# A vision-tower kernel on one core: low-rank coefficients and lora_b as scaled fp16 halves, transposed by DMA

## The reference, cut to what matters

```python
def reference(x, log_dt, B, inv_A_real, A_imag, attn_W, attn_b, W, b, A, Bm, Wr):
    h = s4d_kernel(log_dt, C=x, B, inv_A_real, A_imag, L=1024)     # (32, 128, 1024)
    h = h + layernorm(h) @ attn_W.T + attn_b
    z = layernorm(h)
    gates = softmax(z @ Wr.T)                                      # 4 experts
    proj = einsum('bsi,eri->bser', z, A)                           # 4 experts x rank 8
    lora_out = einsum('bser,eor->bseo', proj, Bm)
    mix = einsum('bse,bseo->bso', gates * 2.0, lora_out)
    return h + (z @ W.T + b) + mix
```

## Time and profile before

| what | value |
|---|---|
| median of 3 runs | 821.04 us |
| the profiled execution's own time | 821.13 us |
| its span in the profile | 819.3 us |
| TensorE busy (PE) | 777.7 us, 95% |
| VectorE busy (DVE) | 625.9 us, 76% |
| ScalarE busy (ACT) | 527.2 us, 64% |
| GpSimd busy (POOL) | 6.5 us, 1% |
| DMA packets of the SP queue | 40.0% of 16 engines |

### The profile page before, as it was taken

One profiled execution on the slowest core, in us unless ns is written; L12 is line 12 of the kernel. 1 busy time (PEld: TensorE's weight loads), 2 busy tenths in 40 slices (PEclk: granted clock), 3 DMA queues, 4 the chain that ended last, 5 costly groups with the idle time before them and its releaser, 6 DMA issues.

```text
span 819.3 us, 14989 instructions
## 1 busy us (share of the span) xinstructions
PE 777.7 (95%) x5390; PEld 389.9 (48%) x5390; DVE 625.9 (76%) x1250; ACT 527.2 (64%) x884; POOL 6.5 (1%) x21
## 2 busy tenths in 40 slices
PE   2758789999999999999999999999999999999998
PEld 2634344444444444444444444444444444444443
DVE  6679797877788778777787778777887787778532
ACT  5667786757676676767766675767757676765210
POOL 2000000000000000000000000000000000000000
PEclk9979999999999999999999999999999999999999
DMA  7837652545233333433324333433324243423223
GB/s 284 288 65 121 131 101 61 98 78 90 58 72 75 77 77 70 96 77 68 80 59 88 65 82 77 95 65 76 72 64 93 54 96 77 89 53 70 59 52 77
DMA packets 185708, 72.28 MB, mean 88 GB/s; under 512 B 174096, under 2 KB 179088, under 8 KB 185560
## 3 DMA queue, kind: packets, MB, share of 16 engines
q1 hardware_dynamic: 185592, 71.90, 40.0%
q10 hardware_dynamic: 96, 0.13, 0.0%
HBM read 14.06 MB, written 16.78 MB: 38 GB/s over the span
## 4 chain that ended last, share of the span: by engine, by line
PE 88%; DVE 5%; ACT 3%; SPq 2%; DMA 1%; issue 1%; DVEq 0%; ACTq 0%
PE ps_g L485 39%; PE ps_g L545 38%; PE ps_a L476 6%; PE ps_g L556 2%; PE ps_g L676 1%; DMA bias_bc<-in_L_attn_bias 1%; PE ps_p L533 1%; SPq L346 1%; DVE wa_lo L1271 1%; SPq L399 1%; PE ps_p L535 1%; DVE stage L1279 0%; DVE x_tok L1172 0%; PE ps_p L550 0%; DVE h_tok L1141 0%
## 5 line engine op out<-in xcount | busy, mean ns | idle before, releaser
L485 PE MATMUL ps_g<-wa_hi,x 128*128 128x512 f16 x1024 | 271.3, 381 | 2.2 <-DMA x<-x_tok 1.9
L545 PE MATMUL ps_g<-wf_hi,x 128*128 128x512 f16 x992 | 265.6, 380 | 0.0
L485 PEld LDWEIGHTS ps_g<-wa_hi,x 128*128 128x128 f16 x1024 | 97.9, 98 | 123.2 <-issue 7.7
L485 PE MATMUL ps_g<-wa_lo,x 128*128 128x512 f16 x512 | 154.2, 380 | 0.0
L545 PE MATMUL ps_g<-wf_lo,x 128*128 128x512 f16 x496 | 149.4, 380 | 0.0
L545 PEld LDWEIGHTS ps_g<-wf_hi,x 128*128 128x128 f16 x992 | 95.1, 98 | 106.7 <-issue 1.8
L1242 DVE SCALAR_TENSOR_TENSOR result<-ps_g,unscale,h_tok 128x1024 f32<-128x1024 f32 x31 | 39.8, 1284 | 84.2 <-PE ps_g L556 84.2
L747 ACT ACTIVATE junk<-ps_a,stat 128x1024 bf16<-128x1024 f32 x32 | 35.6, 1113 | 79.1 <-DVE stat L1144 79.1
L485 PEld LDWEIGHTS ps_g<-wa_lo,x 128*128 128x128 f16 x512 | 50.3, 98 | 60.5 <-issue 0.6
L545 PEld LDWEIGHTS ps_g<-wf_lo,x 128*128 128x128 f16 x496 | 48.5, 98 | 58.6 <-issue 0.6
L753 ACT ACTIVATE junk<-h_tok,stat 128x1024 bf16<-128x1024 f32 x32 | 36.7, 1148 | 60.3 <-DVE stat L1184 60.3
(11 more groups left out here) (208 smaller groups left out, 919.3 us busy)
## 6 DMA issues: line engine op xcount, KB each, us to landing
out<-result SPq DMA_DIRECT2D x124, 128.0 KB, 2.1
stage<-in_L_ffn_W SPq DMA_DIRECT2D x8, 512.0 KB, 13.3
x_raw<-in_x SPq DMA_DIRECT2D x38, 64.0 KB
wf_hi<-in_x SPq DMA_DIRECT2D x1, 2048.0 KB, 10.5
h_tok<-in_L_attn_weight SPq DMA_DIRECT2D x2, 512.0 KB, 4.2
x<-in_L_attn_weight SPq DMA_DIRECT2D x2, 512.0 KB, 6.8
result<-in_L_attn_weight SPq DMA_DIRECT2D x2, 512.0 KB, 7.9
x<-x_tok SPq DMA_TRANSPOSE x64, 3.2
```

The costliest lines, as they stand in the source:

```text
L485: mm = pe.matmul(ps[:, o, :], x1_part(part, ps is ps_g2)[:, k, :], ws[:, k, o * HALF:(o + 1) * HALF], start=k == 0 and part == 0 and ws is ...
L545: pe.matmul(ps_g2[:, o, :], xs[:, k, :], ws[:, k, o * HALF:(o + 1) * HALF], start=k == 0 and xs is x2_hi and ws is wf_hi, stop=False)
```

## The change

Five things are done, and every one touches the low-rank end.

- `lora_split`, `lora_t` and `lb` become fp16. So that fp16's range does for them, lora_b and the coefficients get powers of two: `bound_lora_b` sums the squares of lora_b and of the centred bias, `join_bias_top` and the POOL maximum (now over two columns) bound them, and `lora_scales` makes the factors. `gate_begin` multiplies the projections with the factor `lora_down`.
- `turn_lora`, `copy_lora` and `turn_lora_b` (and ScalarE's two copies of `lb`) are gone from TensorE, DVE and ACT. In their place stand DMA transposes in SP's queue: one of 128 x 1024 for `lb`, and one of 128 x 128 for each block.
- `ffn_end` waits for the DMA transpose, and its two matmuls are fp16.
- In the loop DVE runs `gate_end` ahead of `low_u`, and ACT runs `gate_exp` ahead of `high_u`.
- The constant columns of `lora_split` are filled once at the start.

```diff
             def turn_x1(t, i):
...
+            def turn_lora(t, i):
+
+                at_least(sp, s_g2, 2 * t + i)
+                sp.wait_ge(s_soft, 6 * (2 * t + i) + 6)
+                sp.dma_start_transpose(lora_t[:, :].unsqueeze(1), lora_split[:, :]).then_inc(s_lora_t, 16)
+
+            def turn_lora_b():
+
+                sp.wait_ge(s_lbn, 3)
+                sp.dma_start_transpose(lb[:, :, :], lbn_rows.bitcast(F16)).then_inc(s_lbt, 16)
...
-            turn_weights(KB + 1, KB + 5)
+            turn_weights(9, 13)
+            turn_lora_b()
             turn_x2(0, 0)
-            turn_weights(KB + 5, 2 * KB)
+            turn_weights(13, 16)
             load_x(2)
             turn_x1(1, 0)
+            turn_lora(0, 0)
             turn_x2(0, 1)
...
                     if (t, i) != (TILES - 1, 1):
                         turn_x1(*after(t, i))
+                    turn_lora(*before(t, i))
                     turn_x2(t, i)
             t = TILES - 1
+            turn_lora(t, 1)
             store(t, 0)
...
-            def turn_lora(t, i):
-                pe.wait_ge(s_soft, 6 * (2 * t + i) + 6)
-                pe.transpose(ps_p[0:KL, P:2 * P], lora_split[:, :].bitcast(F32), ident[:, :])\
-                    .then_inc(s_lora_t, 1)
-
             def ffn_end(t, i):
-                pe.wait_ge(s_lora_sb, 2 * t + i + 1)
+                pe.wait_ge(s_lora_t, 16 * (2 * t + i + 1))
                 for o in range(2):
-                    mm = pe.matmul(ps_g2[:, o, :], lora_t[:, :], lb[:, o * HALF:(o + 1) * HALF],
-                                   start=False, stop=True)
+                    mm = pe.matmul(ps_g2[:, o, :], lora_t[0:KL, :], lora_rows(o), start=False, stop=True)
                 mm.then_inc(s_g2, 1)
...
-            turn_lora(0, 0)
             turn_x(2)
             ffn_part(0, 0, range(3, KB), (1,))
+            pe.wait_ge(s_lbt, 16)
             ffn_end(0, 0)
...
-                ffn_part(*b, range(0, 6))
-                turn_lora(*b)
-                ffn_part(*b, range(6, KB))
+                ffn_part(*b, range(KB))
                 ffn_end(*b)
...
+            def bound_lora_b():
+
+                dve.wait_ge(s_lb, 16 * (KB + 1))
+                dve.wait_ge(s_bias_dve, 1)
+                rows, squares = params[:, 0:KB * ER], params[:, 780:780 + KB * (ER + 1)]
+                dve.memset(lbn[:, :, KL:P], 0.0)
+                dve.scalar_tensor_tensor(out=squares[:, KB:], in0=rows, scalar=1.0, in1=rows, op0=ALU.mult,
+                                         op1=ALU.mult, accum_out=top[:, 3:4]).then_inc(s_lb_top, 1)
+                dve.tensor_scalar(lbb, lbb, bias_stat[:, 1:2], None, ALU.subtract).then_inc(s_lb_top, 1)
+                dve.wait_ge(s_lb_top, 2)
+                dve.scalar_tensor_tensor(out=squares[:, 0:KB], in0=lbb, scalar=1.0, in1=lbb,
+                                         op0=ALU.mult, op1=ALU.mult, accum_out=bias_square).then_inc(s_lb_top, 1)
+
+            def join_bias_top():
+
+                dve.wait_ge(s_top, 2)
+                dve.wait_ge(s_lb_top, 3)
+                dve.tensor_scalar(top[:, 2:3], bias_square, XSCALE ** -2, top[:, 2:3], ALU.mult, ALU.max)\
+                    .then_inc(s_top, 1)
+
+            def lora_scales():
+
+                dve.wait_ge(s_lb_power, 1)
+                dve.tensor_scalar(lora_power.bitcast(U32), lora_top.bitcast(U32), 1, EXPONENT,
+                                  ALU.logical_shift_right, ALU.bitwise_and).then_inc(s_lb_power, 1)
+                dve.wait_ge(s_lb_power, 2)
+                dve.reciprocal(lora_up, lora_power).then_inc(s_lb_power, 1)
+                dve.tensor_scalar(lora_down, lora_power, ROOT / LORA_POWER, None, ALU.mult).then_inc(s_lb_power, 1)
+                dve.wait_ge(s_lb_power, 4)
+                dve.tensor_scalar(lora_up, lora_up, LORA_POWER / ROOT, None, ALU.mult).then_inc(s_lb_power, 1)
+                dve.wait_ge(s_power, 10)
+                dve.wait_ge(s_lb_power, 5)
+                dve.tensor_scalar(gate_unscale, unscale[:, 1:2], lora_up, None, ALU.mult).then_inc(s_lb_power, 1)
...
             attn_lo(2, 3)
+            bound_lora_b()
             dve.wait_ge(s_lo1, 1)
             weight_norms(1, ps_p[:, 0:P])
+            join_bias_top()
             round_turns(0, 1)
             split_scales(1)
...
             ffn_lo(10, 11, 12)
+            lora_scales()
             split_lora_b()
```

More of the change, by code:

```diff
@@ L126, in program @@
         lora = sb("lora", [P, ER])
-        lora_split = sb("lora_split", [P, KL], F32R)
-        lora_t = sb("lora_t", [KL, P], F32R)
+        lora_split = sb("lora_split", [P, P], F16)
+        lora_t = sb("lora_t", [P, P], F16)
         params = sb("params", [P, 1280])
@@ L139, in program @@
         x2_tok = stage[:, 0, :]
+        bias_square, lora_top, lora_power, lora_down, lora_up, gate_unscale = (lora_stat[:, k:k + 1] for k in range(6))
         x_halves = spare[:, 0:L // 2].bitcast(U16).rearrange("p (i q k) -> p i q k", i=SUB, q=4)
@@ L396, in load_lora_a, with load_weight @@
                 sp.dma_start(rows[ER:G, :], gate_w).then_inc(landed, 16)
[L398 to L402, removed]
+            def load_weight(first, end):
+                for n in range(first, end):
+                    rows = attn_rows[n] if n < KB else ffn_rows[n - KB]
+                    sp.dma_start(raw_block(n), rows).then_inc(s_wload[n], 16)
+            load_weight(0, 3)
+            sp.dma_start(x_all, x.rearrange("c (b h) n r -> (c b) (h n r)", b=4)).then_inc(s_x_all, 16)
+            load_x(0)
+            load_weight(3, 8)
             sp.dma_start(bias_bc[:, :], attn_b.unsqueeze(0).broadcast_to((P, L))).then_inc(s_bias, 16)
-            for n in range(KB, 2 * KB):
-                sp.dma_start(raw_block(n), ffn_rows[n - KB]).then_inc(s_wload[n], 16)
+            load_weight(8, 16)
             sp.wait_ge(s_pre_dve, PRE)
@@ L564, in turn_lora_a @@
                 mm.then_inc(s_wg_t, 1)
[L566 to L573, removed]
             pe.wait_ge(s_const, 3)
@@ L663, in _ @@
             project(t, 0)
-            ffn_part(t, 0, range(0, 6))
-            turn_lora(t, 0)
-            ffn_part(t, 0, range(6, KB))
+            ffn_part(t, 0, range(KB))
             ffn_end(t, 0)
@@ L677, in _ @@
                                   start=k == 0 and part == 0 and ws is wf_hi, stop=False)
-                pe.wait_ge(s_lora_sb, 2 * TILES)
-                pe.matmul(ps_g1[:, o, :], lora_t[:, :], lb[:, cols], start=False, stop=True).then_inc(s_g2_last, 1)
+                pe.wait_ge(s_lora_t, 16 * 2 * TILES)
+                pe.matmul(ps_g1[:, o, :], lora_t[0:KL, :], lora_rows(o), start=False, stop=True).then_inc(s_g2_last, 1)
         @block.scalar
@@ L896, in step @@
                 rstd_guess(t, i, stat_2, s_ssq2, s_log2, s_y2)
+                gate_exp(*before(t, i))
                 if waves:
                     high_u(t + 1, i)
-                gate_exp(*before(t, i))
                 high_2(t, i)
@@ L965, in top_over_partitions @@
             def top_over_partitions(k):
-                pool.wait_ge(s_top, k + 1)
-                pool.partition_all_reduce(top[:, k, 1:2], top[:, k, 0:1], P, bass.bass_isa.ReduceOp.max)\
-                    .then_inc(s_wall, 1)
+                if k == 0:
+                    pool.wait_ge(s_top, 1)
+                    one, everywhere = top[:, 0:1], top[:, 1:2]
+                else:
+                    pool.wait_ge(s_top, 3)
+                    pool.wait_ge(s_lb_top, 1)
+                    one, everywhere = top[:, 2:4], top[:, 4:6]
+                pool.partition_all_reduce(everywhere, one, P, bass.bass_isa.ReduceOp.max).then_inc(s_wall, 1)
             pool.wait_ge(s_pre_dve, EXPS + 26)
@@ L989, in tt @@
                 link(dve.tensor_tensor, o, a, b, op)
-            for tile, value in ((ones[:, :], 1.0), (half_pi[:, :], pi / 2), (quarter[0:N, :], 0.25),
+            for tile, value in ((half_pi[:, :], pi / 2), (quarter[0:N, :], 0.25),
                                 (quarter[N:P, :], 0.0), (eps[:, :], EPS), (steps_a[:, 0:1], 0.5),
+                                (lora_split[:, :], BIAS_COLUMN),
                                 (steps_a[:, 1:2], 1.0)):
@@ L1203, in gate_begin @@
                 dve.wait_ge(s_proj, 2 * t + i + 1)
-                dve.tensor_copy(proj[:, :], ps_p[:, 0:G]).then_inc(s_proj_sum, 1)
+                dve.tensor_scalar(proj[:, :], ps_p[:, 0:G], lora_down, None, ALU.mult).then_inc(s_proj_sum, 1)
                 dve.wait_ge(s_proj_sum, 2 * (2 * t + i) + 1)
-                dve.tensor_tensor(proj[:, :], proj[:, :], ps_p[:, G:2 * G], ALU.add).then_inc(s_proj_sum, 1)
+                dve.scalar_tensor_tensor(out=proj[:, :], in0=ps_p[:, G:2 * G], scalar=lora_down, in1=proj[:, :],
+                                         op0=ALU.mult, op1=ALU.add).then_inc(s_proj_sum, 1)
                 dve.wait_ge(s_proj_sum, 2 * (2 * t + i) + 2)
@@ L1229, in gate_end @@
```

(15 more changed lines are left out.)

64 lines of the change are left out of this document (34 added, 30 removed).

## The result

The changed kernel takes 825.14 us (median of 7 runs, 824.13 to 827.24), the kernel before, on the same chip, 821.16 us (7 runs, 821.02 to 821.95): a ratio of 1.0052, with a 95% interval of 1.0038 to 1.0066. It is 4.0 us slower. The forecast was 823.0: the direction was right, and the time lies just inside the upper edge of the range, 825.2, but the loss is twice the 1.9 us forecast.

What follows compares the result with a forecast made beforehand. TensorE bounds the loop; ahead of it the set-up chain runs through DVE, ACT and SP. 821.13 - 4.5 (loop) + 6.1 (set-up) + 0.5 (end) = 823.2, stated as 823.0 us, range 820.2 to 825.2.

Steps and rivals of the forecast that it cites:

- The loop: TensorE's work per block: no transpose and a shorter fp16 pair save 0.145 us a step, 4.5 us in all.
- the rival of 7.4 us: Faster: fp16 weight loads also free what follows the pair, the loop saves 7.4 us, total 817.4; chance 0.09.
- The end: Last block: the new DMA ahead of turn_x2(15, 1) delays project and the last coefficients, +0.5 us.
- The set-up: Everything ahead of the loop, up to s4(1, 1): 4.2 + 1.6 + 0.3 = +6.1 us.
- Step 1: Set-up, DVE: bound_lora_b stands on the chain ahead of ScalarE's sine and adds 1.3 us.
- Step 2: Set-up, DVE: lora_scales, five small operations less the constants no longer written, adds 0.7 us.
- Step 3: Set-up, to low_1(1, 0): gate_end no longer delays keep_h(1, 0), which starts at 95.95, +1.45; SP released at 106.65.
- step 5: Set-up, granted clock: half clock for 3.3 us behind the new wait costs 1.6 us, plus 0.3 at project(0, 0).
- ScalarE's give-back: Set-up, ACT: without its copies of lb it gives back about 1 us.
- Step 4: Set-up, ffn_end(0, 0): coefficients issued behind turn_x1(1, 0), TensorE waits 4.2 us, s4(1, 1) starts at 110.85, +4.2.
- The term of 0.3 for the wait at project(0, 0): Set-up: that wait grows to about 5.5 us, a longer stretch at the lower clock adds 0.3 us.
- The rivals: Alternative outcomes; the one meant: the new wait comes but the clock stays full, 821.6, no change; chance 0.30.

Runs made afterwards that it cites:

- c0: The changed kernel itself, measured again on another chip: 825.02 us, ratio 1.0035 to the kernel before.
- b1: The kernel before plus 14 matmuls that nothing reads, ahead of project(0, 0): 822.02 us, ratio 0.9997 to the kernel before.
- e7: e1 with bound_lora_b, lora_scales and split_lora_b moved on DVE and lora_b's transpose moved behind load_x(2) on SP: 817.81 us, ratio 0.9948 to the kernel before.
- e9: e7 with bound_lora_b in another place, behind round_turns(0, 1): 817.33 us, ratio 0.9950 to the kernel before.
- e1: The changed kernel with the first block's coefficient transpose issued ahead of turn_x1(1, 0) in SP's queue: 821.16 us, ratio 0.9989 to the kernel before.
- e4: The changed kernel without bound_lora_b, join_bias_top and lora_scales, constants for their factors: 822.74 us, ratio 1.0005 to the kernel before.
- e2: The changed kernel plus 20 matmuls that nothing reads, between ffn(0, 0) and ffn_end(0, 0): 822.78 us, ratio 1.0010 to the kernel before.
- e10: e9 plus filler matmuls ahead of turn_weight(4) and (6), and the last block's x2(15, 1) transposes issued before lora_t(15, 0): 815.82 us, ratio 0.9924 to the kernel before.

## Why the prediction was right or wrong

**The loop: right.** 0.143 us a step, forecast 0.145. The DMA transposes landed 2.3 us from issue in the median, with 2.4 taken, and no step waited; the weight loads of fp16 gave nothing beyond the pair, which rules out the rival of 7.4 us.

**The end: right.** 709.10 - 705.3 is 3.8 us; 30 steps of 0.143 are 4.3; so the end adds 0.5. The forecast was 0.5 less the 0.15 that the last block's own pair and transpose save, 0.35. project(15, 1) waited 0.5 us, where 0.2 to 0.3 was forecast:

```profile
810.41 0.21 PE L559 MATMUL ps_p<-wg,x 128*128 128x72 f16 x1 [0.51 <-DMA x<-stage]
```

**The set-up: +6.1 forecast.** On the medians it is 4.0 + 3.8 = 7.8 us on the first chip and 3.1 + 3.8 = 6.9 on the chip of c0.

- Step 1, bound_lora_b: 1.01 us, forecast 1.3. Step 2, lora_scales: from s4(0, 1) to the `stage` of ffn block 13 it is 78.08 - 61.15 = 16.93 us, before 74.43 - 58.40 = 16.03: 0.90, forecast 0.7. Together 1.9 of 2.0.
- Step 3, the step that failed: "project(0, 0) starts at 89.8" and keep_h(1, 0) at 95.95. They were at 92.56 and 99.52, 3.6 us late, and in c0, near the median run, at 91.52 and 98.29, 2.3 us late. The step moved both by DVE's additions alone. It put at nothing what TensorE at half the clock costs ahead of x2(0, 0), and, but for the 0.3 of step 5, it took the landing of x2 and TensorE's work behind it to be as long as before. The runs showed three things in their place. The low half of x2 was issued at 87.92 (c0: 86.98), where 86.3 was forecast. It landed in 4.5 us (4.4) for 3.4, with the pause of the DMA traffic in it. And project and ffn took 4.65 us for 4.12 and s4(1, 0) 2.23 for 1.93, which is 0.8 us (0.6 in c0).
- The first of the three in detail: 0.70 us lie ahead of keep_h(0, 0) (0.38 in c0) and 1.04 between wa_hi and s4(0, 1) (0.50 in c0). Of the 0.70, 0.34 is a turn of weights that took 1.43 us for 1.09 with the clock at 0.50 for 1.00, and 0.36 lies still further ahead and is not explained; the 1.04 is TensorE at half the clock. b1 has 2.10 and 0.82 in the same places without the change, so they are at least in part chance. Is there a cost of the change in the 1.04? Ahead of turn_weight(6) DVE's additions made TensorE's wait 4.4 for 3.3 us, and behind 4.3 and more it took 1.97 us in each trace, behind 3.3 it took 1.26, 1.42 and 1.97. But it also took 1.97 behind 3.54 in e7 and behind 2.74 in e9. So that is a guess which the runs do not settle.
- ScalarE's give-back, which I had as 1 us, was there: in e1, e4 and e7, which have the short landing, it is 9.4, 9.2 and 9.6 us from the issue of x2's low half to keep_h(1, 0), 10.4 before and 11.6 in the changed kernel.
- Step 4, the new wait: from the end of low_1(1, 0) at 110.24 to s4(1, 1) in the chain, 115.05, it is 4.8 us, forecast 4.2; the landing was right (2.39 for 2.4), and 0.5 is the pair at half the clock, which is also part of step 5's 2.1. e1 shows that the order of SP's queue is the cause.
- Step 5, the clock behind that wait: mis-sized, 2.1 us (e2) for 1.6. The term of 0.3 for the wait at project(0, 0) was 0.8 (the third of the three above), and was on the path only since x2 was late; b1 shows nothing for it. The rivals say that no row lies between a wait of 2.07 us, with the full clock behind it, and one of 3.80. The trace of before has two: behind 2.70 us, at 28.42, the clock was 1.00 until 30, and behind 3.31 us it was 0.50 from 54 on. The second speaks for the fall that was forecast:

```profile
53.03 1.26 PE L523 MATMUL ps_g<-ident,result 128*128 128x128 f32 x8 [3.31 <-DVE wa_lo L1271]
```

```profile
54.00:54.50 0.50, 0.50 (x3) 0.17 (x2) 0.47 (x2) 0.11 (x1) 0.00 (x0) 0.50 0.00 0
```

On both traces of the changed kernel the failed step carries most: keep_h(1, 0) was 3.6 us late to the forecast, and s4(1, 1) 4.1; in c0 it was 2.3 and 2.9. Yet on the medians only 0.8 to 1.7 us of set-up are missing from the forecast, of which e2 explains about 0.5. The kernel before has such stretches at half the clock too, and on the other chips its medians are 0.6 to 0.9 us above the one that I forecast from. How much of step 3's lateness the change causes, and how much is the draw of one execution, stays open. That the time still fell inside the range is owed to the width of the range, not to the sum.

The page "VectorE: DVE Perf Modes" of the Trainium skill, section "Rules for kernel authors", says to use TensorE for 128 x 128 where a result in PSUM will do. In the loop the trace speaks against it, since TensorE bound there and the DMA was hidden. The 1,309 ns of the section "The three transpose paths" are not what TensorE waited for, 2.39 us from issue to landing. In the set-up e1 shows that the place in the queue cost, and not the DMA transpose.

## What to carry to other kernels

When a small transfer replaces work on an engine, its place in the in-order queue is part of the change: ask what the instruction ahead of it waits for, in the prologue too, where loop order does not hold; here moving one line was worth 3.8 us. A wait of TensorE can be paid twice, once in itself and once in the clock behind it (here 5.6 and 2.1 us), but the second only where TensorE is on the path: b1's filling gave nothing and e2's 2 us. One profiled execution is one draw of such a set-up; set two or three beside each other before a difference of 1 us at one place is given to the change.

## What was not expected of the hardware

- The same program's set-up shows the half clock in different places from run to run: s4(0, 0), at 33 us, took 1.91 us in most traces, 3.17 in b1 and 3.07 in e10, long ahead of any edit of b1. The kernel before ranges over 0.9 us on the first chip and over 4.4 on that of e1; that the places of the half clock make this spread is likely, not shown.
- The pause of DMA traffic at 89 to 94 us, with about 285 GB/s right behind it where 205 is usual.
- A 128 x 128 fp16 transpose by DMA holds SP's queue for 1.12 us in the loop, nearly as long as the 1.24 to 1.34 of one eight times as large, and lands 2.3 us from issue, against 3.1 to 3.2 in the median.
